# Attention values in one dense block per head pair, read by 64-row products, against a block-diagonal copy read by 128-row products

## What is computed

```python
q = proj(query, Wq, bq); k = proj(key, Wk, bk); v = proj(value, Wv, bv)   # [b, H=16, s, dk=16]
scores = einsum('bhqd,bhkd->bhqk', q, k) / sqrt(dk)
bid = arange(s) // 64
scores = scores + where(bid[:, None] == bid[None, :], 0.0, NEG)
attn = softmax(scores, axis=-1)
x = einsum('bhqk,bhkd->bhqd', attn, v)                                    # the change is here
x = x.transpose(0, 2, 1, 3).reshape(b, s, d) @ Wo + bo
...
x = x + xattn(layernorm(x), ctx, ctx, ...)
x = x + moe(layernorm(x), gate_w, expert_bias, w_up, w_down)
```

## Time and profile before

| what | value |
|---|---|
| median of 3 runs | 843.11 us (842.78 to 844.79) |
| span of the profiled execution | 841.2 us |
| what lies around the span (median less span) | 1.9 us |
| PE busy | 738.7 us (88% of the span) |
| DVE busy | 561.5 us (67%) |
| POOL, ACT busy | 443.2 us (53%), 363.6 us (43%) |
| L430, probabilities times values | 512 matmul records, 60.9 us busy; 512 load records |

### The profile page before, as it was taken

One profiled execution on the slowest core, in us unless ns is written; L12 is line 12 of the kernel. 1 busy time (PEld: TensorE's weight loads), 2 busy tenths in 40 slices (PEclk: granted clock), 3 DMA queues, 4 the chain that ended last, 5 costly groups with the idle time before them and its releaser, 6 DMA issues.

```text
span 841.2 us, 20449 instructions
## 1 busy us (share of the span) xinstructions
PE 738.7 (88%) x6144; PEld 665.2 (79%) x6145; DVE 561.5 (67%) x1215; ACT 363.6 (43%) x657; POOL 443.2 (53%) x584
## 2 busy tenths in 40 slices
PE   4999999999999934599999999999999999999300
PEld 4899999999999832288989999999999999898200
DVE  4899898998989758565555555555555555554195
ACT  2777777777777711122222222222222222222185
POOL 3677777777777623534444444444444444432287
PEclk9999999999999965589999999999999999999755
DMA  4233333233232110011111111111111111110494
GB/s 154 94 103 107 114 98 108 99 106 112 96 115 91 51 39 0 25 39 52 52 51 50 50 50 44 44 50 50 45 49 44 50 50 50 50 37 26 144 312 169
DMA packets 39874, 64.52 MB, mean 77 GB/s; under 512 B 5408, under 2 KB 30240, under 8 KB 39840
## 3 DMA queue, kind: packets, MB, share of 16 engines
q1 hardware_dynamic: 31632, 42.37, 15.7%
q0 software_dynamic: 7488, 20.46, 7.6%
q10 hardware_dynamic: 720, 1.26, 0.4%
HBM read 45.46 MB, written 18.61 MB: 76 GB/s over the span
## 4 chain that ended last, share of the span: by engine, by line
PE 87%; DVE 4%; issue 3%; POOL 2%; DMA 1%; ACT 1%; SPq 0%; DVEq 0%; POOLq 0%; ACTq 0%
PE ps_a L527 25%; PE ps_b L541 24%; PE ps_a L387 7%; PE ps_b L430 7%; PE ps_c L409 3%; PE ps_c L414 3%; PE ps_b L397 3%; PE ps_a L465 3%; PE ps_a L452 2%; PE ps_c L495 2%; PE ps_c L511 2%; PE ps_a L476 1%; PE ps_c L377 1%; PE ps_a L440 1%; PE ps_c L422 1%
## 5 line engine op out<-in xcount | busy, mean ns | idle before, releaser
L527 PE MATMUL ps_a<-area,w_hi 128*128 128x256 f16 x1248 | 208.8, 274 | 1.7 <-DVE area L792 1.7
L541 PE MATMUL ps_b<-w_hi,area 128*128 x1248 | 206.4, 273 | 0.0
L1052 POOL DMA_INDIRECT y_rows<-area x78 | 78.0, 1001 | 209.2 <-ACT area L937 197.3
L527 PE MATMUL ps_a<-area,w_lo 128*128 128x256 f16 x624 | 171.1, 274 | 0.0
L541 PE MATMUL ps_b<-w_lo,area 128*128 x624 | 170.1, 273 | 0.0
L932 ACT ACTIVATE area<-ps_a 128x512 f32<-128x512 f32 x156 | 93.2, 598 | 143.1 <-PE ps_a L527 141.7
L527 PEld LDWEIGHTS ps_a<-area,w_hi 128*128 x1248 | 122.8, 98 | 16.4 <-issue 2.1
L541 PEld LDWEIGHTS ps_b<-w_hi,area 128*128 128x128 f16 x1248 | 122.1, 98 | 14.1
L790 DVE TENSOR_SCALAR area<-ps_c 128x512 f16<-128x512 f32 x39 | 27.0, 692 | 151.7 <-PE ps_c L511 151.7
L802 DVE SCALAR_TENSOR_TENSOR area<-area 128x512 f16<-128x512 f32 x156 | 108.3, 694 | 5.4
L1042 POOL DMA_INDIRECT area<-xn_rows,area x78 | 77.7, 996 | 46.9 <-issue 35.9
(11 more groups left out here) (130 smaller groups left out, 1263.8 us busy)
## 6 DMA issues: line engine op xcount, KB each, us to landing
area<-weights SPq DMA_DIRECT2D x32, 512.0 KB, 3.3
w_hi<-y_rows SPq DMA_DIRECT2D x32, 256.0 KB, 4.6
resid<-x_in SPq DMA_DIRECT2D x32, 128.0 KB, 2.1
area<-ctx_t SPq DMA_DIRECT2D x32, 128.0 KB, 2.1
xn_rows<-area SPq DMA_DIRECT2D x32, 128.0 KB, 1.7
out<-w_lo SPq DMA_DIRECT2D x16, 256.0 KB, 2.7
area<-xn_rows,area POOLq DMA_INDIRECT x78
y_rows<-area POOLq DMA_INDIRECT x78
```

Source lines behind the costliest of these rows:

```text
L527: mm = pe.matmul(ps_h[:, q, (ic % 2) * SLOTS:(ic % 2 + 1) * SLOTS], w[:, bass.ds(first + (hc * I + ic * P), P)], r[b][:, hc, :], start=(n ...
L541: mm = pe.matmul(ps_y[:, b, v * D:(v + 1) * D], g[b][:, ic, v * P:(v + 1) * P], w[:, bass.ds(first + (EXPERT_COLS + ic * D), D)], start=(n ...
L1052: pool.indirect_dma_start(y_rows[:, :], bass.IndirectOffsetOnAxis(ap=didx[b][:, v:v + 1], axis=0), y_s[b][:, v * D:(v + 1) * D], None).the ...
```

## The change

`v_x` becomes dense: 33 columns for every head pair (two heads and the ones), with keys of block 0 in partitions 0 to 63 and keys of block 1 in partitions 64 to 127, and no zeros. The product of a head pair becomes two, one per block: each loads 64 rows of `prob_t` (all 128 columns) and streams 33 columns of 64 rows. A tile has 16 such products. Blocks alternate in the order, and block 0 writes to bank 0 of `ps_b`, block 1 to bank 1. ACT copies values in one operation over 128 partitions, DVE normalizes in two operations of 64 partitions by 256 elements, and the two memsets of zeros are gone. The counts of the semaphores follow; no wait is added, and no operation changes its place among the others.

```diff
-        v_x = [carve(PAIRS * NB * VCOLS).rearrange("p (s c b x) -> p s c b x", s=STRIPS, c=HC, b=NB) for _ in range(2)]
+        v_x = [carve(PAIRS * VCOLS).rearrange("p (s c x) -> p s c x", s=STRIPS, c=HC) for _ in range(2)]
...
-        ps_o = ps_b[:, :, 0:4 * NB * VCOLS].rearrange("p a (y x) -> p a y x", x=VCOLS)
+        ps_o = ps_b[:, :, 0:PAIRS * VCOLS].rearrange("p b (y x) -> p b y x", x=VCOLS)
...
                     for h in range(PAIRS):
-                        mm = pe.matmul(ps_o[:, h // 4, (h % 4) * NB:(h % 4 + 1) * NB, :], prob_t[:, h, :],
-                                       v_x[b][:, h // HC, h % HC, :, :], start=True, stop=True)
+                        for n in range(NB):
+                            r = slice(n * BLOCK, (n + 1) * BLOCK)
+                            mm = pe.matmul(ps_o[:, n, h, :], prob_t[r, h, :], v_x[b][r, h // HC, h % HC, :], start=True, stop=True)
...
-            dve.memset(v_x[0], 0.0).then_inc(zeroed, 1)
-            dve.memset(v_x[1], 0.0).then_inc(zeroed, 1)
             dve.memset(k_bd.rearrange("p c b s k -> p (c b s k)"), 0.0).then_inc(zeroed, 1)
-            dve.wait_ge(zeroed, 3)
+            dve.wait_ge(zeroed, 1)
             for b in range(2):
-                for n in range(NB):
-                    r = slice(n * BLOCK, (n + 1) * BLOCK)
-                    ins = dve.memset(v_x[b][r, :, :, n, 2 * DK:VCOLS].rearrange("p s c x -> p (s c) x"), 1.0)
-            ins.then_inc(zeroed, 1)
+                dve.memset(v_x[b][:, :, :, 2 * DK:VCOLS].rearrange("p s c x -> p (s c) x"), 1.0).then_inc(zeroed, 1)
...
                     for h in range(2):
                         r = slice(h * BLOCK, (h + 1) * BLOCK)
-                        for m in range(NB):
-                            dve.tensor_tensor(o_n[r, m, :].rearrange("p (a y d) -> p a y d", a=2, d=DK),
-                                              ps_o[r].rearrange("p a (y b) x -> p a y b x", b=NB)[:, :, :, m, h * DK:(h + 1) * DK],
-                                              o_sum[r].rearrange("p (a y b) -> p a y b", a=2, b=NB)[:, :, :, m:m + 1].to_broadcast([BLOCK, 2, 4, DK]),
-                                              ALU.mult).then_inc(o_r, 1)
+                        dve.tensor_tensor(o_n[r].rearrange("p b (y d) -> p b y d", d=DK), ps_o[r, :, :, h * DK:(h + 1) * DK],
+                                          o_sum[r].rearrange("p (b y) -> p b y", b=NB).unsqueeze(3).to_broadcast([BLOCK, NB, PAIRS, DK]),
+                                          ALU.mult).then_inc(o_r, 1)
...
-                    for n in range(NB):
-                        r = slice(n * BLOCK, (n + 1) * BLOCK)
-                        act.activation(v_x[b][r, :, :, n, 0:2 * DK],
-                                       ps_v[r].rearrange("p (c s d) -> p s c d", c=HC, s=STRIPS),
-                                       ACT.Copy, scale=1.0 / (CTX_SCALE * W_SCALE)).then_inc(v_r, 1)
+                    act.activation(v_x[b][:, :, :, 0:2 * DK], ps_v.rearrange("p (c s d) -> p s c d", c=HC, s=STRIPS),
+                                   ACT.Copy, scale=1.0 / (CTX_SCALE * W_SCALE)).then_inc(v_r, 1)
```

More of the change, by code:

```diff
@@ L367, in _ @@
             pe.wait_ge(small_in, 16)
-            pe.wait_ge(zeroed, 4)
+            pe.wait_ge(zeroed, 3)
             def step(j, u):
@@ L394, in step @@
                     pe.wait_ge(p_r, t + 1)
-                    since(pe, o_r, 4 * t)
+                    since(pe, o_r, 2 * t)
                     for h in range(PAIRS):
@@ L419, in step @@
                 if valid(t):
-                    pe.wait_ge(o_r, 4 * (t + 1))
+                    pe.wait_ge(o_r, 2 * (t + 1))
                     for n in range(NB):
@@ L427, in step @@
                     pe.wait_ge(pt_r, t + 1)
-                    pe.wait_ge(v_r, 2 * (t + 1))
+                    pe.wait_ge(v_r, t + 1)
                     for h in range(PAIRS):
-                        mm = pe.matmul(ps_o[:, h // 4, (h % 4) * NB:(h % 4 + 1) * NB, :], prob_t[:, h, :],
-                                       v_x[b][:, h // HC, h % HC, :, :], start=True, stop=True)
+                        for n in range(NB):
+                            r = slice(n * BLOCK, (n + 1) * BLOCK)
+                            mm = pe.matmul(ps_o[:, n, h, :], prob_t[r, h, :], v_x[b][r, h // HC, h % HC, :], start=True, stop=True)
                     mm.then_inc(o_ps, 1)
@@ L437, in rows_for_gate @@
                         since(pe, x2t_r, t)
-                        since(pe, v_r, 2 * (min(t + 3, TILES) if isinstance(t, int) else t + 3))
+                        since(pe, v_r, min(t + 3, TILES) if isinstance(t, int) else t + 3)
                         for c in range(HC):
@@ L447, in step @@
                     pe.wait_ge(ctx_lo_r, t + 1)
-                    since(pe, v_r, 2 * t)
+                    since(pe, v_r, t)
                     n = 0
@@ L663, in step @@
                     since(dve, ot_ps, t)
-                    since(dve, o_r, 4 * t)
-                    dve.reciprocal(o_sum.rearrange("p (a y) -> p a y", a=2), ps_o[:, :, :, 2 * DK]).then_inc(osum_r, 1)
+                    since(dve, o_r, 2 * t)
+                    dve.reciprocal(o_sum.rearrange("p (b y) -> p b y", b=NB), ps_o[:, :, :, 2 * DK]).then_inc(osum_r, 1)
                     dve.wait_ge(osum_r, t + 1)
@@ L846, in _ @@
             act.wait_ge(small_in, 16)
-            act.wait_ge(zeroed, 4)
+            act.wait_ge(zeroed, 3)
             def step(j, u):
```

## The result

| | before | changed |
|---|---|---|
| median | 842.94 us (4 runs, 842.18 to 844.79) | 850.47 us (4 runs, 849.34 to 851.05) |
| ratio | 1 | 1.0091 (95%: 1.0072 to 1.0110) |
| span of the profiled execution | 841.2 us | 849.2 us |
| PE busy | 738.7 us | 746.9 us |
| DVE, ACT busy | 561.5, 363.6 us | 556.5, 351.2 us |

The time lies inside the range (846 to 917) and on the forecast side. The forecast was +16 us; measured are +7.5. The two spans are 8.0 apart, and PE's busy time grew by 8.2: what was added is work or waiting inside PE's rows, not a new idle stretch.

A forecast was written before the change was run, and what follows sets the result against it. PE was taken to bound the attention part, with L430 paced by its loads. Span 841.2 + 0 (loads) + 17.0 (passages) - 0.7 (start) = 857.5, with 1.9 around it 859.4 us; range 846 to 917.

The forecast's parts named there:

- Loads side by side: Value products: 32 loads of 64 rows fill 16 slots of 0.111 us, cost 0; forecast case, chance 0.50.
- Passages: Into and out of the value products, both load overlaps are lost: 0.53 us a tile, 17 us over 32 tiles.
- Start: Kernel start: memsets of zeros gone, ones halved; gain between 0 and 1.2 us, taken as 0.7.
- Cover within a pair: Value products: 33-column streams might be laid bare, at most 0.44 us a tile, 14 us in all; taken as 0.
- DVE and ACT: Attention steps: DVE's normalization about 0.2 us less, ACT's two copies become one; nothing gained in the steady steps.
- A: Value products: loads go one after another, 57 us more; 899.4 us without passages, 916.4 with them; chance 0.31.
- D: Value products: granted clock falls and a load costs twice as much, 112 us over 32 tiles, about 1010 us; chance 0.06.
- B: Value products: loads side by side and no price for changing shape, 842.4 us; chance 0.09.
- C: Value products: a 64-row load costs half and two run at once; DVE becomes the bound, 823 us; chance 0.04.
- Signs in the profile: Profile after: L432's loads in pairs within 0.111 us, DVE's reduction wait growing with the step, experts unchanged to 0.3 us a group.

The follow-up runs named there:

- the halves in turn: Changed kernel with its product loops exchanged, eight products of block 0, then eight of block 1: 972.49 and 990.36 us.
- an added pair: Changed kernel with one extra 128-row transpose amid a tile's products, making two more changes of array shape: 865.82 us, ratio 1.0272.
- the halved scores: Kernel before, value products untouched, each score product (L387) cut into two of 64 rows and 128 columns on alternating halves: 830.01 us, ratio 0.9854.
- the second execution: The changed kernel run once more without edits, to see whether the stretch at the lower clock belongs to the change: 849.98 us, ratio 1.0103.

## Why the prediction was right and where it was off

- **Loads side by side: right.** It was taken as one of two ends, 0 or 57 us, at odds of 0.50 to 0.31 and without a row that could decide, so part of it is luck; 1024 loads in 59.6 us show 0. Of the reasons that the prediction gave, the alternation of blocks is shown to be needed (the halves in turn lose the pairs), and the separate banks are not tested.
- **Passages: the step that failed, by its size.** 0.53 us a tile were charged, both overlaps lost whole; the trace has 0.317, and an added pair 0.31. The mechanism is right: the first load of a new shape waits for the stream of the old one. Two things were taken too large. The load starts 0.07 to 0.08 us ahead of the (modelled) end of the last matmul, at L432, L441 and at the halved scores alike, so 0.26 and 0.27 of overlap shrink to 0.07 and 0.08, a loss of 0.38. And 0.06 comes back behind the crossing: L441's first load to L453's is 163.95 - 163.78 = 0.17 us in place of 0.23, by the loads of the kernel before below. 0.38 - 0.06 = 0.32. The Trainium skill, "TensorEngine Tiling (Array Packing)", section Tiling Modes, says that a change of mode drains the engine. The trace agrees up to those 0.07 to 0.08 us, and what it costs here, with PE's queue full, is 0.32 us there and back. 32 tiles at 0.317 make 10.1 in place of 17.0, and that is most of the miss. The loads of the kernel before at that place:

```profile
159.79 0.26 PEld L440 LDWEIGHTS ps_a<-cst,area 128*128 128x128 f32 x2
160.02 0.64 PEld L452 LDWEIGHTS ps_a<-area 128*128 128x128 f16 x6
```

- **Only part of the steps paid it.** The prediction took all 32. The first four steps paid 0.06 in all in one execution and 0.33 in the other, in place of 1.27, because PE waited there in part and because the clock rose earlier, and the restarts of the loop gave back 0.5. The sum had neither.
- **Start: 0.7 charged, 0.24 measured at the first transposes (0.19 in the second execution).** The prediction named the landing of the input as the unknown, and it is what bounds now: the memsets end 1.43 us earlier (2.09 against 3.52), and 1.23 of it is spent waiting. DVE's start in the changed kernel, against the earlier trace rows:

```profile
2.01 0.08 DVE L571 MEMSET area<- 128x8 f32 x2
3.32 0.43 DVE L589 BATCH_NORM_STATS2 area<-resid 128x6 f32<-128x256 f32 x1 [1.23 <-DMA resid<-x_in]
```

- **Cover within a pair: 0, as taken.** The loads keep 0.111 us with streams of 33 columns.
- **DVE and ACT: hidden in the steps**, shown by undoing them (9.02 both ways). Two DVE operations take 0.88 us where some 0.8 was estimated. What that experiment lost behind the attention part stays open.
- **Tail: not priced, about 1.5 us back behind the attention part.** 0.8 of it lies in the experts, where the clock rises again 5.7 us after their first product before (356.7 us, earlier than the 364 given above for the end of the routing) and 4.1 us after it (366.2) in the changed kernel; 0.6 lies in the last pass. The change's part in either is not shown.
- **Rivals.** A (one after another) and D (the clock) fell for the changed kernel and both occur in the halves in turn: 1.36 us a tile and a mean clock of 0.76. B (no passages) fell by the added pair. C's condition, a cheaper load, fell (188 against 192 ns), but its bound by DVE was met by the halved scores.
- **Signs in the profile:** the loads of L432 start in pairs, and the experts take 427.5 us for 39 groups against 428.2, 0.02 us a group. The wait of DVE ahead of its reduction did not grow; it came ahead of L582.

The account of the second execution of the changed kernel, whose clock stayed at its upper level from 20 to 310 us: 841.2 - 0.2 (start) + 8.2 (31 steps) + 0.2 (last tiles) - 1.4 (behind them) = 848.0 us of span, its own.

## What to carry to other kernels

Cutting a product over 128 rows into two over 64 makes two loads and two streams that run side by side, if products next to each other in the order are on different halves (and, in all runs here, on different banks); in turn the loads took 3.22 us in place of 1.86, and the clock fell on top. What a group of products gains by it is set by what bounds it: nothing where the loads do (1.78 us of loads stayed 1.78), much where the stream does (the scores went from 1.73 to 1.09 us, the way out included), and each visit to the other shape costs 0.32 us of a full PE. So look first whether a group's pace changes with its columns, then count the changes of shape, and then ask which engine is next: here DVE left 0.25 of the 0.49 us.

## What the hardware showed that was not expected

- Paired loads start 6 to 7 ns apart, and four loads of the other half were pulled beside the last four at the seam of the halves in turn.
- The granted clock fell to 0.50 with PE's records busy without a gap: in turns with 1.00 in the halves in turn, and five times for 3.4 us within the steps with 16 products of 128x33 (32 loads) a tile. With 32 loads in pairs it held through the steps from 20 us on; in the last tiles there are single pieces of 3.4 us, which one execution of the changed kernel has (1.3 us) and another has not.
- A change between products over 128 and over 64 rows costs 0.09 to 0.10 us going in and 0.22 coming out, the same for streams of 33 and of 128 columns in the first part (0.094 and 0.10).
